# A two-layer sequence model on one Trainium2 core: masks, weight loads and weight preparation moved into the mixers' block

## What is computed

```python
x = x + attn_L0(cond_L0(x, ...))      # the mixer: a state-space scan behind the conditioner
x = x + ffn_L0(cond2_L0(x, subject))  # a mixture of 8 experts, 2 for each token
```

```python
ctx      = causal_ema(x, tau_ctx)                     # h = alpha * h + x_t along the tokens
gate     = sigmoid([x, ctx] @ Wg + bg)
mod      = sigmoid(gelu(x @ Wn1 + bn1) @ Wn2 + bn2)   # 8 rows of 512
traces   = [causal_ema(x * gate * (mod_d + 0.5), tau_d) for d in range(8)]
temporal = sum(traces[d] * softmax(blend)[d])
soma     = gelu(x @ Wsoma + bsoma)
out      = (soma * sigmoid(temporal @ Wtemp + btemp)) @ Wout
y        = layernorm(out) * gamma + beta
```

## Time and profile before

| | |
|---|---|
| median of 3 runs | 3955.41 us (3953.57 to 3958.09) |
| the profiled execution | 3959.05 us |
| its span, first to last instruction | 3957.3 us |
| mean granted TensorE clock | 0.937 |
| TensorE busy | 3352.7 us, 85% |
| VectorE busy | 2400.7 us, 61% |
| ScalarE busy | 1483.9 us, 37% |
| GpSimd busy | 631.0 us, 16% |

### The profile page before, as it was taken

One profiled execution on the slowest core, in us unless ns is written; L12 is line 12 of the kernel. 1 busy time (PEld: TensorE's weight loads), 2 busy tenths in 40 slices (PEclk: granted clock), 3 DMA queues, 4 the chain that ended last, 5 costly groups with the idle time before them and its releaser, 6 DMA issues. The chain is left out here.

```text
span 3957.3 us, 36159 instructions
## 1 busy us (share of the span) xinstructions
PE 3352.7 (85%) x10476; PEld 1680.7 (42%) x10477; DVE 2400.7 (61%) x2992; ACT 1483.9 (37%) x2754; POOL 631.0 (16%) x753
## 2 busy tenths in 40 slices
PE   4778787878787877569979999999999999978991
PEld 2333333333333333236644444444444444436770
DVE  4599999999999999922222343534344443443335
ACT  1535353535353534223323242423333232413440
POOL 0000202020202020223320010101101010116771
PEclk9899898989898989779989999999999999989995
DMA  2122222222222222242230000000101010044447
GB/s 80 49 69 80 79 80 79 80 79 79 79 79 79 80 74 81 75 177 66 66 120 22 20 34 25 29 32 21 47 6 53 1 53 3 28 177 144 153 146 274
DMA packets 160129, 296.56 MB, mean 75 GB/s; under 512 B 27392, under 2 KB 84352, under 8 KB 158720
## 3 DMA queue, kind: packets, MB, share of 16 engines
q1 hardware_dynamic: 136048, 234.45, 18.5%
q0 software_dynamic: 20352, 57.17, 4.0%
q10 hardware_dynamic: 3600, 3.35, 0.3%
HBM read 200.72 MB, written 94.16 MB: 75 GB/s over the span
## 5 line engine op out<-in xcount | busy, mean ns | idle before, releaser
L1151 PE MATMUL ps<-hs,ident 128*128 128x512 f32 x1024 | 539.4, 676 | 239.7 <-DVE hs L1260 239.7
L1254 DVE TENSOR_TENSOR_SCAN hs<-dA,hs 128x2048 f32<-128x2048 f32 x128 | 565.4, 4417 | 6.7
L407 POOL COPY rows<-new_slot 128x64 f32<-128x64 f32 x48 | 25.5, 561 | 2826.3 <-DVE new_pl L533 2803.6
L1811 PE MATMUL ps<-pT,V 128*128 128x512 f32 x1024 | 450.5, 593 | 7.0 <-DVE pT L1974 7.0
L1209 ACT ACTIVATE dA<-dl,w_An 128x511 f32<-128x511 f32 x512 | 326.0, 709 | 339.0 <-DVE hs L1254 337.4
L1151 PEld LDWEIGHTS ps<-hs,ident 128*128 128x128 f32 x1024 | 215.5, 217 | 550.8 <-DVE hs L1260 284.5
L1246 DVE TENSOR_TENSOR hs<-u,bb 128x2048 f32<-128x2048 f32 x128 | 292.4, 2285 | 12.2 <-PE ps L1151 11.7
L1260 DVE TENSOR_TENSOR hs<-hs,cb 128x2048 f32<-128x2048 f32 x128 | 290.0, 2266 | 0.0
L1383 POOL DMA_INDIRECT slots<-og,idt x232 | 241.8, 1042 | 273.0 <-DVE og L1471 198.0
L1811 PEld LDWEIGHTS ps<-pT,V 128*128 128x128 f32 x1024 | 189.6, 190 | 223.4 <-issue 214.8
L403 POOL DMA_INDIRECT sorted<-rows,new_pl x192 | 265.1, 1380 | 63.8 <-issue 45.0
(11 more groups left out here) (310 smaller groups left out, 5039.6 us busy)
## 6 DMA issues: line engine op xcount, KB each, us to landing
bb<-bcd SPq DMA_DIRECT2D x128, 256.0 KB, 3.5
cb<-bcd SPq DMA_DIRECT2D x128, 256.0 KB, 3.3
xg<-sorted SPq DMA_DIRECT2D x232, 136.0 KB, 2.1
slots<-zeros SPq DMA_DIRECT2D x136, 128.0 KB, 3.2
mb<-modd SPq DMA_DIRECT2D x64, 256.0 KB, 4.1
qrg<-slots SPq DMA_DIRECT2D x16, 1024.0 KB, 8.7
rg<-slots SPq DMA_DIRECT2D x32, 256.0 KB, 4.6
w_Lr<-in_Lora SPq DMA_DIRECT2D x8, 576.0 KB, 3.9
```

The costliest lines, as they stand in the source:

```text
L1151: ins = pe.matmul(ps[:, j, :], ident[:, :], m.hs[:, N % 3, j, :], start=False, stop=(N % NS == NS - 1))
L1254: dve.tensor_tensor_scan(state, m.dA[:, N % 2].rearrange("p j t -> p (j t)"), state, 0.0, ALU.mult, ALU.add).then_inc(s_h, 1)
L1811: ins = pe.matmul(ps[:, 6 + j, :], V[:, m, h * D + j * P:h * D + (j + 1) * P], pT[:, i % 2, h % 2, m, :], start=(h == 0 and m == 0), stop= ...
```

## The change

The first two blocks are gone. Their work is in the streams of the mixers' block:

- GpSimd makes the masks first (`make_masks`); TensorE, ScalarE and VectorE wait for all 15 steps.
- SP loads x of sample 0 first, then the weights in two groups with a semaphore each: `f.first` (9 DMAs: `tau` twice, `vec`, `Wn1`, `Wg`, `Wn2`, `blend`, `Wsoma`, `bn2`) and `f.rest` (11 DMAs). The 11 scratch DMAs come behind the eighth spread of `mod` and before x of sample 1, and SP waits for them at the block's end.
- The preparation is cut in parts. Ahead of step 0 of the first conditioner: alpha and the blend's exponent. Ahead of step 3: the rest but the negation of `An`, which VectorE does ahead of step 7. TensorE's 16 products of `setup_pe` stand ahead of its step 3, and it then waits for all of VectorE's part 1.

```diff
+        def load_first_weights(sp, f):
+            sp.dma_start(f.tau[:, 0:NTR], a["tau"].partition_broadcast(P)).then_inc(f.first, 16)
+            sp.dma_start(f.tau[:, NTR:NTR + 1], a["tau_ctx"].partition_broadcast(P)).then_inc(f.first, 16)
+            for t, name in f.loads:
+                sp.dma_start(t[:], a[name]).then_inc(f.first, 16)
+            sp.dma_start(bn2[:, :], a["bn2"].rearrange("(d o) -> d o", o=1)).then_inc(f.first, 16)
+            for t, name in f.more:
+                sp.dma_start(t[:], a[name]).then_inc(f.rest, 16)
+            sp.dma_start(bg0[:, :], a["bg0"].partition_broadcast(P)).then_inc(f.rest, 16)
+        def setup_pe(pe, f):
+            pe.wait_ge(f.rest, f.n_rest)
+            for j in range(2 * JI):
+                product(pe, ps[:, 0, 2 * j:2 * j + 2],
+                        [(Win[:, i, j * P:(j + 1) * P], beta[:, i:i + 1].to_broadcast([P, 2])) for i in range(DC)], f.shift)
+        def setup_act(act, f, part):
+            if part == 0:
+                act.wait_ge(f.exps, 1)
+                act.activation(alpha[:, :], f.tau[:, :], ACT.Exp).then_inc(f.exps, 1)
+                act.wait_ge(f.exps, 3)
+                act.activation(f.blend[:, :, :], f.blend[:, :, :], ACT.Exp).then_inc(f.exps, 1)
+            else:
+                act.wait_ge(f.rest, f.n_rest)
+                act.activation(An[:, :, :], An[:, :, :], ACT.Exp).then_inc(f.exps, 1)
+                act.wait_ge(f.shift, 2 * JI)
...
+        def setup_dve(dve, ch, f, part):
+            blend, bl1 = f.blend, f.bl1
+            if part == 0:
+                dve.wait_ge(f.first, f.n_first)
+                dve.tensor_scalar(f.tau[:, :], f.tau[:, :], 87.0, None, ALU.min).then_inc(f.exps, 1)
+                ch.link(dve.tensor_reduce(bl1[:, :], blend[:, :, :], X, ALU.max))
+                dve.wait_ge(f.exps, 2)
...
+            elif part == 1:
+                dve.wait_ge(f.exps, 4)
...
+                dve.wait_ge(f.rest, f.n_rest)
...
@@ -1095,8 +1099,10 @@
                     load_x(0)
+                    load_first_weights(sp, f)
                     store_mod(sp, c, 0)
                     spread_mod(sp, c, 0, range(NTR))
+                    clear_scratch(sp)
                     load_x(1)
                     store_rows_bc(sp, c, 0)
@@ -1167,7 +1175,14 @@
+                    pe.wait_ge(masks, MASKS)
+                    pe.wait_ge(f.first, f.n_first)
                     for n in range(NS):
+                        if n == 3:
+                            setup_pe(pe, f)
+                            pe.wait_ge(f.su, f.steps - 1)
+                        if n == 8:
+                            pe.wait_ge(f.scaled, 1 + DC)
                         cond_pe(pe, n, c, 0)
                         ahead_pe(pe, n, m, 0)
@@ -1209,9 +1224,14 @@
+                    act.wait_ge(masks, MASKS)
+                    setup_act(act, f, 0)
                     for n in range(NS):
+                        if n == 3:
+                            setup_act(act, f, 1)
                         cond_act(act, n, c, 0)
                         ahead_act(act, n, m, c, 0)
+                    act.wait_ge(f.su, f.steps)
                     decays(0)
@@ -1272,7 +1292,14 @@
+                    su = Chain(dve, f.su)
+                    dve.wait_ge(masks, MASKS)
+                    setup_dve(dve, su, f, 0)
                     for n in range(NS):
+                        if n == 3:
+                            setup_dve(dve, su, f, 1)
+                        if n == 7:
+                            setup_dve(dve, su, f, 2)
                         cond_dve(dve, n, c, cc, 0)
                         ahead_dve(dve, n, m, c, ch, 0)
```

More of the change, by code:

```diff
@@ L154, in build @@
         scratch = sem("scratch_cleared")
[L155 to L185, removed]
@@ L188, in load_first, with clear_scratch @@
+        def clear_scratch(sp):
+            sp.wait_ge(masks, 1)
+            for M in (M0, M1):
+                sp.dma_start(M.sorted[M.spare:M.spare + P, :], zeros[:, :]).then_inc(scratch, 16)
+            for q in range(TT * K0):
+                sp.dma_start(M0.pairs[N * K0 + P * q:N * K0 + P * (q + 1), :], zeros[:, 0:D]).then_inc(scratch, 16)
+            sp.dma_start(M0.weight[B], zeros[:, 0:TT * K0]).then_inc(scratch, 16)
         def load_first(st):
@@ L217, in load_first @@
             Dc = sb("Dc", [P, JI, 4, P])
[L218 to L224, removed]
@@ L291, in load_first @@
-            return (Wg, Wn1, Wn2, Wsoma, Wtemp, WoutC, Win, bin_, Wxd, Wxbc, Wdt, Wo, Wg0, bg0, vec, cw, An, alpha, bn2,
-                    mix, Dg, Dc, h1, dts)
+            f = Tensors()
+            f.first, f.rest = sem("first_weights_loaded"), sem("mixer_weights_loaded")
+            f.su, f.exps = sem("setup_step"), sem("setup_exps")
+            f.shift, f.scaled = sem("setup_input_shift"), sem("setup_input_scaled")
+            f.loads = [(vec, "vec"), (Wn1, "Wn1"), (Wg, "Wg"), (Wn2, "Wn2"), (blend, "blend"), (Wsoma, "Wsoma")]
@@ new lines, in load_first @@
+            f.more = [(WoutC, "Wout"), (cw, "cw"), (Wtemp, "Wtemp"), (Win, "Win"), (Wxd, "Wxd"), (Wxbc, "Wxbc"),
+                      (Wdt, "Wdt"), (An, "Araw"), (Wo, "Wo"), (Wg0, "Wg0")]
+            f.n_first, f.n_rest = 16 * (len(f.loads) + 3), 16 * (len(f.more) + 1)
+            f.steps = 3 + 3 + DC * NTR + 2 + 5 * JI + 2 + DC + 1
+            f.tau, f.blend, f.bl1, f.cw = tau, blend, bl1, cw
+            return (Wg, Wn1, Wn2, Wsoma, Wtemp, WoutC, Win, bin_, Wxd, Wxbc, Wdt, Wo, Wg0, bg0, vec, cw, An, alpha, bn2,
+                    mix, Dg, Dc, h1, dts, f)
@@ new lines, in setup_pe @@
+        def setup_pe(pe, f):
[13 more added lines that the diff above has]
+                act.wait_ge(f.shift, 2 * JI)
+                act.activation(bin_[:, :].unsqueeze(2),
+                               ps[:, 0, 0:4 * JI].rearrange("p (j o) -> p j o", o=2)[:, :, 0:1], ACT.Copy).then_inc(f.scaled, 1)
+                for i in range(DC):
+                    act.activation(Win[:, i, :], Win[:, i, :], ACT.Copy, scale=gamma[:, i:i + 1]).then_inc(f.scaled, 1)
+                act.wait_ge(f.scaled, 1 + DC)
```

110 lines of the change are left out of this document (48 added, 62 removed).

## The result

The changed kernel took 3923.39 us, median of 6 runs (3910.09 to 3934.26); the kernel before took 3958.84 in the same rounds. The ratio, which leaves out one run of the kernel before that took 6346.91 us, is 0.9915, 95% interval 0.9903 to 0.9926: faster by 0.85%, about 34 us. The forecast was 3927.2, within 3922.5 to 3937.0.

A forecast was written before the change was run, and what follows sets the result against it. VectorE bounds the mixers' loop, TensorE the attention, no engine the first 36 us. Gate product 29.9 us earlier, less 0.1, 1.0 and 0.6, gives 28.2, so the median goes from 3955.41 to 3927.2 us, range 3922.5 to 3937.

The forecast's parts named there:

- x and the first weights: Start of the head: engines have x and the first nine weight DMAs at 8.5 us, between 7.0 and 10.2.
- Rival B: Head's loads: the first weights land with all the others, at about 17 us; gain 19.7 us, 3935.7; chance 0.08.
- Alpha: VectorE and ScalarE before the context scans: 2.4 us from the first weights, so the scans start at 10.9 us.
- Preparation on VectorE: Between context scans and `gated`: 9.7 us of work fits in some 9.8 us of gap; cost 0.1 us.
- Preparation on TensorE: `setup_pe` behind the soma products: 4.0 to 7.0 us, stalling the third trace's scans 0 to 3.1; taken as 1.0.
- The clock before that: Gate product behind a 1.2 us gap: its passes may run slowly, costing 0 to 2.4 us; taken as 0.6.
- Behind the gate: Rest of the first conditioner: every row as before, no further gain or loss.
- ScalarE and the scratch: First conditioner: about 4 us of moved ScalarE work and 4.8 us of scratch DMAs are covered; cost nothing.
- C: Gate and soma products: TensorE stays at the lower clock for 26 passes; gain about 19 to 20, 3936; chance 0.07.
- D: Start of the mixers' loop: a wait for something unmoved swallows the gain; 3953 to 3957; chance 0.02.
- E: Attention: the shift in time lowers TensorE's clock, losing more than 28 us, so the kernel is slower; chance 0.03.
- and the loop behind it as well: Mixers' loop behind the conditioner: every row as before, no gain or loss there.

The follow-up runs named there:

- e4_all_weights: The changed kernel with TensorE and VectorE waiting at the start for all twenty weight transfers, not the first nine; 3927.34 us, ratio 0.9929.
- e1_again: The changed kernel run again with no edit; 3914.39 us, ratio 0.9897.
- e6_prepare_first: The changed kernel with all preparation but the negation of An ahead of step 0 of the first conditioner; 3940.23 us, ratio 0.9951.
- e15_queue_nudge: The changed kernel with tau and blend loads on ScalarE's queue, early Exp table, Wsoma loaded later, and a needless VectorE operation before the first state scan; 3908.91 us.
- e14_before_nudge: The kernel before with one needless VectorE operation ahead of the first state scan; 3953.89 us, ratio 0.9992.

## Why the prediction was right, step by step

**x and the first weights**: seen at 8.95, forecast 8.5, inside 7.0 to 10.2. (The 1.5 us in the sum for the lower end were taken from no row, and no run shows them.) x went out at 0.78 and the last of the nine at 5.32, as forecast (0.8, 5.3); from there to use it took 3.6 us, near a single transfer's 3.3 and not the 4.9 behind a backlog. Rival B is refuted by `e4_all_weights`.

**Alpha**: 8.96 to 11.37 is 2.4, as forecast. **The gate product** came 29.4 us earlier, forecast 29.9.

**Preparation on VectorE**: hidden, with 1.64 us of idle time left before `gated` where the forecast had it fit by 0.1; a part of that room is the slower gate product's (1.3 us, below). In `e1_again`, with the fast one, there is none: ScalarE's `wg` was ready at 22.71, and VectorE went from its last preparation step straight to `gated` at 22.93. There the work fills the gap to within 0.2 us, as forecast. `e6_prepare_first` shows what the cover is worth.

**Preparation on TensorE**: the term was mis-sized, 1.0 against nothing. The passes took 3.63 us and not 4.0 to 7.0, and the third trace's scans kept `gated`'s 28.1. What the Trainium skill says on the page "TensorE: Matmul & The Clock Gate", Part 1, that activity frees the array from its lower clock, gave a stall near 0, and the durations agree: 6.96 us at the head (`e6_prepare_first`), 3.63 behind dense passes, and no stall. The granted clock doesn't tell the two apart, it is 1.00 in both.

**The clock before that**: forecast 0.6 within 0 to 2.4. The difference from 29.4 to 28.1 is 1.3 in this execution, and `e1_again` has none of it (`gated` 30.0 us earlier): a term that varies by run. The granted clock of 1.00 in the stretch from 13.77 to 17.77 us doesn't show it; the passes' durations (3.78 us for four) do.

**Behind the gate**: "from there every row of the conditioner is as before" failed by one row. The `WoutC` product took 5.40 us where it took 3.70, as its window's clock of 0.76 says (1.00 before), and 28.0 became 26.5. `e1_again` has 29.7 there. The forecast's 28.2 lies between the two. The product of before:

```profile
93.04 3.70 PE L373 MATMUL ps<-gated,w_WoutC 128*128 128x512 f32 x8 [2.11 <-DVE gated L859]
```

**ScalarE and the scratch**: hidden as forecast. `go` waits 24.78 us at 58.08 where it waited 29.75, so the 5 us of moved work cost nothing.

**Rivals**: C did not come about; only some passes ran slowly, not 26. D and E neither: the attention's clock is 1.00 and its 392 us are unchanged.

**What failed** is "and the loop behind it as well". The loop took 17.8 us less in the profiled execution, 4.2 of which were lost again right behind it. Of the 34 us between the kernels, 28 are the head, by like groups of runs, and the rest is that 6 of 11 runs of the changed kernel are in the short group against 12 of 78 before. That the median lies so near the forecast is in part luck: with three runs in each group it is the mean of 3918.20 and 3928.59, a time that no run had. The forecast's own sum fits the long group (3958.2 less 28.2 is 3930.0, measured 3930.6); the short group, its 3914.4 and the profiled 3918.20, is below the range's 3922.5, and so is the median of `e1_again`. That the clock's falls set the rhythm is read from the windows above, no run shows it alone. Whether and why the change shifts the mix stays open too: the last fall of the clock before the loop is 0.1 to 0.5 us nearer to it in the long profiles, but `e6_prepare_first` (52.7) and `e15_queue_nudge` (14.9), both with a loop between the two, the half-and-half of `e14_before_nudge`, and samples of both kinds in one execution show that this distance alone does not decide.

## What to carry to other kernels

When blocks stand one behind the other with a barrier, add up what each waits for (here scratch, weights, x), ask for the first consumer's data first with its own semaphore, and put preparation into the first gap of the engine that does it: the landing times and gaps of the old trace gave 28.2 us, and two profiles have 26.5 and 29.7, like groups of runs 28. A phase behind the changed place is unchanged only in its work: if its period is close to a wait for an engine whose clock steps, take several profiles and compare runs group by group before a gain in it is believed or explained. A change of 0.4% there needs more than three runs, since one kernel's own runs lie 16 us apart.

## What was not expected of the hardware

- The same program has two rhythms in its loop, 194.5 to 195.0 and 197.3 to 198.2 us a sample, and can change between them in the middle of an execution; its total times lie 16 us apart with nothing between them in eleven runs.
- 32 passes of 2 columns, each with its weight load, took 6.96 us at the head and 3.63 us behind dense passes, with a granted clock of 1.00 in both.
- Small DMAs on a second queue, issued by 2.2 us, were used at 7.92 us, hardly ahead of the large ones on the first (8.27).
